# Attention on one Trainium2 core: probabilities split query-major and transposed by DMA, applied four slots later

## The chip, the cores and the metric

The kernel runs on one core of one Trainium2 chip (trn2). The metric is device time in microseconds of that core, the median of several runs; 701.6 us to 703.3 us is one and the same kernel here. A core has TensorE (PE in the rows; PEld is its weight loading), VectorE (DVE), ScalarE (ACT), GpSimd (POOL) and SyncE (SP), each with its own instruction queue, which runs strictly in the order in which it was written. They meet through semaphores. 16 DMA engines move data; in this kernel SyncE issues every transfer.

## The reference, cut to what matters

32 sequences of 256 tokens, 384 channels, 6 heads of 64. Layer norm and ReLU, masked attention, output projection, residual.

```
h = relu(layernorm(x))                        # x: 32 x 256 x 384, f32
q, k, v = heads(h @ Wq + bq), heads(h @ Wk + bk), heads(h @ Wv + bv)
scores = q @ k.T / sqrt(64)
probs = softmax(scores + where(adj, 0, -9e15))
out = x + (concat(probs @ v) @ Wf + bf)
```

## The kernel before

Every matrix product is made from f16 halves: a factor is written as hi + lo, and `three` issues the products hi·hi, hi·lo and lo·hi into one accumulator (PSUM) bank.

**A batch and its units.** The kernel goes through the 32 sequences (here: batches) one after the other. The attention of one batch is cut into six units: unit u takes the query half t = u // 3 (128 queries) and the head pair j = u % 3. For each unit `scores` makes the two 128x256 score tiles of the two heads; `mask_and_max` on VectorE adds the mask, scales, negates and keeps the row's minimum (`least`); `exps` on ScalarE makes f32 probabilities, queries on the partitions. The product with v needs keys on the partitions, so TensorE turns the four 128x128 f32 blocks of the unit with matmuls against an identity (`transpose_probs`, L834) into one of two PSUM banks; ScalarE copies that to f16 as `pt_hi` (L409, scaled by 2^14), VectorE subtracts for `pt_lo` (L543), and `apply_probs` (L850 to L852) accumulates 12 products in the bank `ctx`. A 65th column of ones in v gives the row sum; `divide` divides by it.

**The cycle and its slots.** `cycle(b)` is written out by hand for each engine. It works on batch b's attention, on the projections of batch b+1 and on the end of batch b-1, in six slots that each start with `scores(b, u)`. TensorE turns unit u-1 in slot u and applies unit u-2 in it. Between these stand the projections: `project_qk` in three pairs, `project_v` in two halves, `transpose_h` (L779, turns the normed tokens), `transpose_context` (L860) and `project_out`. Nothing but this written order and the semaphores sets what runs when. Two cycles form the body of the loop.

**The other engines.** GpSimd: `normalise`, `make_mask`, `split_lo` (the lo half of q and k, L354) and `add_bias`. ScalarE moves projections out of PSUM (`qk_full`, `v_hi_part`, `h_hi_part`, `context_hi`). VectorE makes the halves (`qk_hi_part` L559, `v_lo_part`, `h_lo_part`, `context_lo`), the layer-norm statistics (`layer_stats`) and the result (`finish`).

**SyncE.** It loads x and the mask, stores results, and places heads: `scores` contracts a head over 128 partitions, hi on one half and lo on the other, so the split projections must cross partition halves. Four transfers per head pair do this, two of 96 KB within their own partition half (L284) and two of 64 KB to the other half (L285), 12 in a batch. A transfer is issued when the queue reaches it; a wait in the queue holds all that stands behind it.

## Time and profile before

| | us |
|---|---|
| median of 3 runs | 702.35 (701.69 to 703.3) |
| span of the profiled execution | 701.6 |

| engine | busy us, share of the span |
|---|---|
| TensorE | 677.3, 97% |
| VectorE | 555.2, 79% |
| ScalarE | 464.9, 66% |
| GpSimd | 270.1, 39% |
| DMA engines | 33.8% |

Busy time of an engine is the time in which at least one of its instructions is under way. Instructions overlap by their pipelines: a duration in a row is longer than what the instruction costs in a dense sequence. That cost is the distance from its start to the start of the next, and the prediction uses it wherever a timeline shows it.

### The profile page before, as it was taken

What the parts mean: (1) busy time and instruction counts of PE and PEld (TensorE: products, weight loads), DVE (VectorE), ACT (ScalarE), POOL (GpSimd) and SP (SyncE); (2) the same over time, 40 slices, a digit from 0 to 9 for tenths busy, and PEclk for the clock granted to TensorE, in tenths of its full rate; (3) what the DMA queues carried; (4) which work ended last, traced back from release to release, by engine and by line L of the source; (5) the groups of instructions that cost most, each with busy time, mean ns of one, the idle gap of its engine ahead of it and who ended that gap; (6) DMA issues with size and microseconds to landing.
All of it is one profiled execution on the core that took longest, in us unless ns stands there. A gap on an engine that the chain in (4) does not pass through costs nothing.

```text
span 701.6 us, 21244 instructions
## 1 busy us (share of the span) xinstructions
PE 677.3 (97%) x7156; PEld 562.7 (80%) x7156; DVE 555.2 (79%) x1676; ACT 464.9 (66%) x972; POOL 270.1 (39%) x330
## 2 busy tenths in 40 slices
PE   7688999999999999999999999999999999999996
PEld 5466888888888888888888888888888888888874
DVE  5748887887887878788787878878787887888785
ACT  2545676767677676767767676776767677676763
POOL 1334444334444433444443344444334444333420
PEclk8899999999999999999999999999999999999998
DMA  5123333433332343333234333323433332343220
GB/s 187 43 52 89 101 72 89 105 85 90 90 98 71 90 105 84 90 92 96 71 91 105 84 87 94 90 74 94 105 81 89 95 88 75 95 105 78 65 71 35
DMA packets 72453, 61.36 MB, mean 87 GB/s; under 512 B 17649, under 2 KB 72434, under 8 KB 72434
## 3 DMA queue, kind: packets, MB, share of 16 engines
q1 hardware_dynamic: 72434, 61.12, 33.8%
q8 instruction: 11, 0.18, 0.1%
q14 instruction: 8, 0.07, 0.0%
HBM read 17.05 MB, written 12.58 MB: 42 GB/s over the span
## 4 chain that ended last, share of the span: by engine, by line
PE 90%; issue 3%; DVE 3%; DMA 1%; ACT 1%; POOL 1%; SPq 0%; POOLq 0%; DVEq 0%
PE ring L767 17%; PE ring L769 17%; PE ring L768 17%; PE probs_t L834 11%; PE scores L824 6%; PE scores L825 6%; PE ctx L850 3%; PE ctx L852 3%; PE ctx L851 3%; PE ring L779 3%; PE ring L860 3%; DMA w_raw<-in_L_gnn_Wv_dram 1%; ACT probs L404 0%; DMA x_in<-in_x_dram 0%; DVE w_lo L623 0%
## 5 line engine op out<-in xcount | busy, mean ns | idle before, releaser
L404 ACT ACTIVATE probs<-logits,least 128x256 f32<-128x256 f32 x384 | 175.1, 504 | 78.0 <-DVE least L536 77.0
L354 POOL TENSOR_TENSOR split<-qk,split 128x512 f16<-128x512 f32 x96 | 111.3, 1160 | 274.9 <-DVE split L559 274.9
L409 ACT ACTIVATE pt_hi<-probs_t 128x512 f16<-128x512 f32 x192 | 114.6, 597 | 108.1 <-PE probs_t L834 107.3
L536 DVE CUSTOM_DVE_ANT_0 logits<-scores,mask,logit_unscale 128x256 f32<-128x256 f32 x384 | 169.1, 478 | 4.5 <-PE scores L825 3.7
L767 PE MATMUL ring<-h_hi,w_hi 128*128 128x256 f16 x576 | 158.3, 275 | 2.0 <-DVE w_lo L623 1.5
L768 PE MATMUL ring<-h_lo,w_hi 128*128 128x256 f16 x576 | 158.1, 275 | 0.0
L769 PE MATMUL ring<-h_hi,w_lo 128*128 128x256 f16 x576 | 158.0, 274 | 0.0
L543 DVE SCALAR_TENSOR_TENSOR pt_lo<-probs_t,pt_hi 128x512 f16<-128x512 f32 x192 | 131.6, 686 | 0.7 <-ACT pt_hi L409 0.6
L834 PE MATMUL probs_t<-ident,probs 128*128 128x128 f32 x768 | 116.4, 274 | 5.4 <-ACT probs L404 5.3
L559 DVE CAST split<-qk 128x512 f16<-128x512 f32 x96 | 41.3, 430 | 98.3 <-ACT qk L422 98.3
L422 ACT ACTIVATE qk<-ring,qk_bias_s,qkv_ratio 128x256 f32<-128x256 f32 x192 | 96.7, 552 | 15.2 <-PE ring L769 15.2
L824 PE MATMUL scores<-heads 128*128 128x256 f16 x384 | 94.9, 274 | 4.6 <-DMA heads<-split 3.9
L834 PEld LDWEIGHTS probs_t<-ident,probs 128*128 128x128 f32 x768 | 89.9, 141 | 9.4 <-issue 6.5
L362 POOL TENSOR_TENSOR residual<-x_in,bf_full 128x384 f32<-128x384 f32 x64 | 62.7, 1001 | 90.2 <-DVE result L588 83.4
L825 PE MATMUL scores<-heads 128*128 128x256 f16 x384 | 94.5, 273 | 0.0
L851 PE MATMUL ctx<-v_lo,pt_hi 128*128 128x64 f16 x768 | 89.4, 192 | 0.0
L852 PE MATMUL ctx<-v_hi,pt_lo 128*128 128x65 f16 x768 | 89.3, 193 | 0.0
L850 PE MATMUL ctx<-v_hi,pt_hi 128*128 128x65 f16 x768 | 89.2, 194 | 0.0
L850 PEld LDWEIGHTS ctx<-v_hi,pt_hi 128*128 128x128 f16 x768 | 72.1, 97 | 4.4
L851 PEld LDWEIGHTS ctx<-v_lo,pt_hi 128*128 128x128 f16 x768 | 70.9, 98 | 5.5
L852 PEld LDWEIGHTS ctx<-v_hi,pt_lo 128*128 128x128 f16 x768 | 71.0, 97 | 0.0
L767 PE MATMUL ring<-w_hi,ct_hi 128*128 128x384 f16 x192 | 62.8, 327 | 2.2 <-DVE ct_lo L579 2.2
(86 smaller groups left out, 1300.0 us busy)
## 6 DMA issues: line engine op xcount, KB each, us to landing
heads<-split SPq DMA_DIRECT2D x192, 96.0 KB, 2.2
x_in<-in_x_dram SPq DMA_DIRECT2D x32, 384.0 KB, 3.3
heads<-split SPq DMA_DIRECT2D x192, 64.0 KB, 2.1
out_dram<-result SPq DMA_DIRECT2D x64, 192.0 KB, 1.9
adj_in<-in_adj_dram SPq DMA_DIRECT2D x32, 64.0 KB, 2.0
w_raw<-in_L_gnn_Wq_dram SPq DMA_DIRECT2D x1, 576.0 KB, 4.1
w_raw<-in_L_gnn_Wk_dram SPq DMA_DIRECT2D x1, 576.0 KB, 6.5
w_raw<-in_L_gnn_Wv_dram SPq DMA_DIRECT2D x1, 576.0 KB, 6.3
```

Of the source, the lines that this page charges most:

```text
L404: act.activation(probs[u % 2][:, a], logits[u % 2][:, a], ACT.Exp, bias=least[u % 2][:, a:a + 1], scale=-1.0).then_inc(probs_ready, 1)
L536: dve.tensor_tensor_reduce(out=logits[u % 2][:, a], in0=score_bank[u % 2][:, a * S:(a + 1) * S], in1=mask[b.parity][:, t], scale=logit_uns ...
L543: dve.scalar_tensor_tensor(out=pt_lo[u % 2][:].rearrange("p a t q -> p (a t q)"), in0=pt_bank[u % 2][:], scalar=P_SCALE, in1=pt_hi[u % 2][ ...
L767: pe.matmul(out_ap, a_hi, m_hi, start=first, stop=False)
L768: pe.matmul(out_ap, a_hi, m_lo, start=False, stop=False)
L769: return pe.matmul(out_ap, a_lo, m_hi, start=False, stop=last)
L824: pe.matmul(o, q, h[:, 1], start=True, stop=False)
L825: mm = pe.matmul(o, q, h[:, 2], start=False, stop=True)
L834: mm = pe.transpose(pt_bank[u % 2][:, o:o + P], probs[u % 2][:, a, s * P:(s + 1) * P], ident[:])
L850: pe.matmul(ctx_ps[:, h], hi, vh, start=(s == 0), stop=False)
L851: pe.matmul(ctx_ps[:, h, 0:D], hi, vl, start=False, stop=False)
L852: mm = pe.matmul(ctx_ps[:, h], lo, vh, start=False, stop=(s == QT - 1))
```

## The change

The probabilities are no longer turned by TensorE. `exps` takes its bias from `raised` = `least` + ln(2^14), which a new small VectorE instruction makes, so the probabilities come out scaled. Then, still query-major in SBUF, ScalarE copies them to f16 (`p_rows[u][:, 0]`) and GpSimd makes the lo half (`probs_lo`, `p_rows[u][:, 1]`). SyncE issues one DMA transpose per unit, 128 partitions by 1024 f16 values (256 KB), which lands in `p_cols[u]`; `apply_probs` reads that. Each unit has buffers of its own. `apply_probs` of unit u stands in slot u+4 (`LAG`), not u+2.

The two PSUM banks of the turned probabilities join the ring (three banks become five), and many PSUM tiles have another bank. x and the residual have four buffers, the normed halves two. The 64 KB crossing transfers of heads are gone; `copy_heads` makes two VectorE copies in their place for each head pair, from one partition half to the other. All six queues' orders are rewritten, one more cycle runs at the end, and the loop body holds four cycles.

```diff
+        logits = [sb(f"logits{u}", [P, 2, S], F32) for u in range(3)]
+        least = [sb(f"least{u}", [P, 2], F32) for u in range(3)]
+        raised = [sb(f"raised{u}", [P, 2], F32) for u in range(3)]
+        probs = [sb(f"probs{u}", [P, 2, S], F32) for u in range(3)]
+        p_rows = [sb(f"p_rows{u}", [P, 2, 2, S], F16) for u in range(UNITS)]
+        p_cols = [sb(f"p_cols{u}", [P, 2, 2, QT, P], F16) for u in range(UNITS)]
...
-        ring = [bank("ring0"), bank("ring1"), bank("ring2")]
...
+        R_QK = [ring[0], ring[3], ring[2]]
+        R_V = [ring[3], ring[2]]
+        R_CT = [ring[1], ring[4]]
+        R_OUT = [ring[1], ring[4]]
...
-            for k in (-1, 0):
+            for k in range(-1, FIRST_IN_LOOP):
                 cycle(Batch(0, k))
...
-                cycle(Batch(i, 1))
-                cycle(Batch(i, 2))
-            for k in range(2 * TURNS + 1, B + 1):
+                for n in range(RING):
+                    cycle(Batch(i, FIRST_IN_LOOP + n))
+            for k in range(FIRST_IN_LOOP + RING * TURNS, B + 2):
                 cycle(Batch(0, k))
...
             def store(b, t):
                 wait(sp, result_ready, b.count(2, t + 1))
+                alone(sp)
                 sp.dma_start(out_v[b.index(), t], result[t][:]).then_inc(out_stored[t], 16)
             def place_heads(b, j):
                 wait(sp, qk_hi_ready, b.count(C, j + 1))
                 wait(sp, qk_lo_ready, b.count(C, j + 1))
+                alone(sp)
                 for a in range(2):
                     own = slice(D * a, D * a + D)
-                    other = slice(D - D * a, 2 * D - D * a)
                     dst, src = heads[b.parity][:, 2 * j + a], split[j]
                     sp.dma_start(dst[own], src[own, 1:4]).then_inc(heads_placed[j], 16)
-                    sp.dma_start(dst[other, 0:2], src[own, 0:3:2]).then_inc(heads_placed[j], 16)
+            def transpose_probs(b, u):
+                wait(sp, p_lo_ready, b.count(UNITS, u + 1))
+                alone(sp)
+                sp.dma_start_transpose(p_cols[u][:].rearrange("p w a s q -> p (w a s) q"),
+                                       p_rows[u][:].rearrange("p w a k -> p (w a k)")).then_inc(p_placed[u], 16)
...
             def cycle(b):
-                if (b + -1).exists():
-                    store(b + -1, 0)
-                if (b + 3).exists() and (b + 1).exists():
+                here, before, front = b.exists(), (b + -1).exists(), (b + 1).exists()
+                if before:
+                    transpose_probs(b + -1, 4)
+                if b.exists():
+                    place_heads(b, 2)
+                if before:
+                    transpose_probs(b + -1, 5)
+                if here:
+                    transpose_probs(b, 0)
+                if here and (b + 4).exists():
+                    wait(sp, residual_ready, b.count(2, 2))
+                    alone(sp)
+                    load_x(b + 4)
+                if (b + -2).exists():
+                    store(b + -2, 1)
+                if here:
+                    transpose_probs(b, 1)
+                if (b + 3).exists() and front:
                     wait(sp, mask_ready, (b + 1).count(2, 2))
+                    alone(sp)
                     load_adj(b + 3)
                 if (b + 1).exists():
-                    place_heads(b + 1, 0)
-                    place_heads(b + 1, 1)
-                if (b + -1).exists():
-                    store(b + -1, 1)
+                    place_heads((b + 1), 0)
+                if here:
+                    transpose_probs(b, 2)
                 if (b + 1).exists():
-                    place_heads(b + 1, 2)
-                if (b + 3).exists() and (b + 1).exists():
-                    wait(sp, residual_ready, (b + 1).count(2, 2))
-                    load_x(b + 3)
+                    place_heads((b + 1), 1)
+                if here:
+                    transpose_probs(b, 3)
+                if before:
+                    store(b + -1, 0)
...
+            def probs_lo(b, u):
+                wait(pool, p_hi_ready, b.count(UNITS, u + 1))
+                pool.tensor_tensor(p_rows[u][:, 1], probs[u % 3][:], p_rows[u][:, 0],
+                                   ALU.subtract).then_inc(p_lo_ready, 1)
...
+                if here:
+                    split_lo(b, 2)
+                if before:
+                    probs_lo(b + -1, 5)
+                if here:
+                    probs_lo(b, 0)
+                if (b + 2).exists():
+                    normalise(b + 2)
+                if here:
+                    probs_lo(b, 1)
                 if front:
                     make_mask(b + 1)
                     split_lo(b + 1, 0)
...
+                if here:
+                    probs_lo(b, 2)
+                if front:
                     split_lo(b + 1, 1)
-                    if not first:
-                        add_bias(b + 1)
-                if (b + 2).exists():
-                    normalise(b + 2)
-                if front:
...
+                if here:
+                    probs_lo(b, 3)
+                if front:
+                    add_bias(b + 1)
+                if here:
+                    probs_lo(b, 4)
...
             def exps(b, u):
+                wait(act, p_lo_ready, b.count(UNITS, u - 2))
+                wait(act, raised_ready, b.count(UNITS, u + 1))
                 for a in range(2):
-                    wait(act, logits_ready, b.count(2 * UNITS, 2 * u + a + 1))
-                    act.activation(probs[u % 2][:, a], logits[u % 2][:, a], ACT.Exp,
-                                   bias=least[u % 2][:, a:a + 1], scale=-1.0).then_inc(probs_ready, 1)
+                    act.activation(probs[u % 3][:, a], logits[u % 3][:, a], ACT.Exp,
+                                   bias=raised[u % 3][:, a:a + 1], scale=-1.0).then_inc(probs_ready, 1)
             def probs_hi(b, u):
-                wait(act, pt_ready, b.count(UNITS, u + 1))
-                act.activation(pt_hi[u % 2][:].rearrange("p a t q -> p (a t q)"), pt_bank[u % 2][:],
-                               ACT.Copy, scale=P_SCALE).then_inc(pt_hi_ready, 1)
+                wait(act, probs_ready, b.count(2 * UNITS, 2 * u + 2))
+                act.activation(p_rows[u][:, 0], probs[u % 3][:], ACT.Copy).then_inc(p_hi_ready, 1)
...
+                wait(dve, probs_ready, b.count(2 * UNITS, 2 * u - 4))
...
-            def probs_lo(b, u):
-                wait(dve, pt_hi_ready, b.count(UNITS, u + 1))
-                dve.scalar_tensor_tensor(
-                    out=pt_lo[u % 2][:].rearrange("p a t q -> p (a t q)"), in0=pt_bank[u % 2][:],
-                    scalar=P_SCALE, in1=pt_hi[u % 2][:].rearrange("p a t q -> p (a t q)"),
-                    op0=ALU.mult, op1=ALU.subtract).then_inc(pt_lo_ready, 1)
+                        op0=ALU.add, op1=ALU.min, accum_out=least[u % 3][:, a:a + 1]).then_inc(logits_ready, 1)
+                dve.wait_ge(logits_ready, b.count(2 * UNITS, 2 * u + 2))
+                dve.tensor_scalar(raised[u % 3][:], least[u % 3][:], P_RAISE, None, ALU.add).then_inc(raised_ready, 1)
...
+            def copy_heads(b, j):
+                wait(dve, qk_lo_ready, b.count(C, j + 1))
+                for a in range(2):
+                    own = slice(D * a, D * a + D)
+                    other = slice(D - D * a, 2 * D - D * a)
+                    dst, src = heads[b.parity][:, 2 * j + a], split[j]
+                    dve.tensor_copy(dst[other, 0:2], src[own, 0:3:2]).then_inc(heads_copied, 1)
...
                 if here:
                     mask_and_max(b, 0)
+                if before:
+                    divide(b + -1, 0)
                 if front and not first:
                     h_lo_part(b + 1)
-                lo_of(0)
-                if before:
-                    finish(b + -1, 0)
...
                 if here:
                     mask_and_max(b, 1)
-                lo_of(1)
-                if front:
-                    qk_hi_part(b + 1, 0)
+                    copy_heads(b, 2)
+                    v_lo_part(b, 0)
+                    v_lo_part(b, 1)
...
-            def transpose_probs(b, u):
-                wait(pe, pt_lo_ready, b.count(UNITS, u - 1))
-                for a in range(2):
-                    wait(pe, probs_ready, b.count(2 * UNITS, 2 * u + a + 1))
-                    for s in range(QT):
-                        o = (a * QT + s) * P
-                        mm = pe.transpose(pt_bank[u % 2][:, o:o + P], probs[u % 2][:, a, s * P:(s + 1) * P],
-                                          ident[:])
-                mm.then_inc(pt_ready, 1)
             def apply_probs(b, u):
                 t, j = u // C, u % C
-                wait(pe, pt_lo_ready, b.count(UNITS, u + 1))
...
-                        hi, lo = pt_hi[u % 2][:, a, s], pt_lo[u % 2][:, a, s]
+                        hi, lo = p_cols[u][:, 0, a, s], p_cols[u][:, 1, a, s]
                         vh, vl = v_hi[b.parity][:, s, h], v_lo[b.parity][:, s, h]
                         pe.matmul(ctx_ps[:, h], hi, vh, start=(s == 0), stop=False)
...
+                def attend(u):
+                    if here:
+                        scores(b, u)
+                    if u < LAG:
                         if before:
-                            transpose_probs(b + -1, UNITS - 1)
+                            apply_probs(b + -1, UNITS - LAG + u)
                     elif here:
-                        transpose_probs(b, u - 1)
...
+                        apply_probs(b, u - LAG)
+                attend(0)
                 if front and not first:
                     transpose_h(b + 1)
+                if here:
+                    project_v(b, 1)
+                attend(1)
+                if front:
+                    project_qk(b + 1, 0)
+                attend(2)
+                if before:
+                    transpose_context(b + -1, 0)
+                if front:
+                    project_qk(b + 1, 1)
+                attend(3)
+                if b.k == 1:
+                    pe.wait_ge(w_lo_ready, 10)
                 if before:
                     project_out(b + -1, 0)
-                if here:
...
-                if front:
...
+                    project_qk(b + 1, 2, (0,))
...
+                attend(4)
+                if before:
+                    transpose_context(b + -1, 1)
+                if front:
+                    project_qk(b + 1, 2, (1,))
+                    project_v(b + 1, 0, (0,))
+                attend(5)
+                if front:
+                    project_v(b + 1, 0, (1, 2))
                 if before:
                     project_out(b + -1, 1)
-                apply_of(3)
```

The order of the instructions shows this at three places. First TensorE, the start of a slot behind the loop, before (`probs_t` is the PSUM bank of turned probabilities, `ident` the identity):

```order
L824 MATMUL scores<-heads 128x256
L825 MATMUL scores<-heads 128x256
L824 MATMUL scores<-heads 128x256
L825 MATMUL scores<-heads 128x256
L834 MATMUL probs_t<-ident,probs 128x128 x4
L767 MATMUL ring<-h_hi,w_hi 128x256
L768 MATMUL ring<-h_lo,w_hi 128x256
```

and after, the same place:

```order
L874 MATMUL scores<-heads 128x256
L875 MATMUL scores<-heads 128x256
L874 MATMUL scores<-heads 128x256
L875 MATMUL scores<-heads 128x256
L890 MATMUL ctx<-v_hi,p_cols 128x65
L891 MATMUL ctx<-v_lo,p_cols 128x64
L892 MATMUL ctx<-v_hi,p_cols 128x65
```

The row of four transposes (L834) is gone between the scores and what follows.

GpSimd, one batch behind the loop, before (`split` is the lo half of q and k, `residual` is x plus bias):

```order
L348 TENSOR_SCALAR mask<-adj_in,mask_scale 128x256 x2
L354 TENSOR_TENSOR split<-qk_0,split 128x2x256
L354 TENSOR_TENSOR split<-qk_1,split 128x2x256
L362 TENSOR_TENSOR residual<-x_in,bf_full 128x384 x2
L334 TENSOR_TENSOR rstd<-var_s,half 128x2
L339 TENSOR_SCALAR normed<-x_in,neg_mean,rstd 128x384 x2
L354 TENSOR_TENSOR split<-qk_2,split 128x2x256
```

and after:

```order
L391 TENSOR_TENSOR split<-qk_2,split 128x2x256
L405 TENSOR_TENSOR p_rows<-probs,p_rows 128x512 x2
L371 TENSOR_TENSOR rstd<-var_s,half 128x2
L376 TENSOR_SCALAR normed<-x_in,neg_mean,rstd 128x384 x2
L405 TENSOR_TENSOR p_rows<-probs,p_rows 128x512
L385 TENSOR_SCALAR mask<-adj_in,mask_scale 128x256 x2
L391 TENSOR_TENSOR split<-qk_0,split 128x2x256
L405 TENSOR_TENSOR p_rows<-probs,p_rows 128x512
L391 TENSOR_TENSOR split<-qk_1,split 128x2x256
L405 TENSOR_TENSOR p_rows<-probs,p_rows 128x512
L400 TENSOR_TENSOR residual<-x_in,bf_full 128x384 x2
L405 TENSOR_TENSOR p_rows<-probs,p_rows 128x512
```

Six instructions on `p_rows` have come in between, and the batch starts with `split` of its own third head pair, which before stood last.

SyncE, the queue of one batch behind the loop, before:

```order
L274 DMA out_dram<-result 128x384
L284 DMA heads<-split 64x768
L285 DMA heads<-split 64x2x256
L284 DMA heads<-split 64x768
L285 DMA heads<-split 64x2x256
L284 DMA heads<-split 64x768
L285 DMA heads<-split 64x2x256
L284 DMA heads<-split 64x768
L285 DMA heads<-split 64x2x256
L274 DMA out_dram<-result 128x384
L284 DMA heads<-split 64x768
L285 DMA heads<-split 64x2x256
```

and after:

```order
L298 DMA_TRANSPOSE p_cols<-p_rows 128x8x128
L292 DMA heads<-split 64x768 x2
L298 DMA_TRANSPOSE p_cols<-p_rows 128x8x128 x2
L274 DMA x_in<-in_x_dram 128x2x384
L282 DMA out_dram<-result 128x384
L298 DMA_TRANSPOSE p_cols<-p_rows 128x8x128
L277 DMA adj_in<-in_adj_dram 128x2x256
L292 DMA heads<-split 64x768 x2
L298 DMA_TRANSPOSE p_cols<-p_rows 128x8x128
L292 DMA heads<-split 64x768 x2
L298 DMA_TRANSPOSE p_cols<-p_rows 128x8x128
L282 DMA out_dram<-result 128x384
```

Twelve head transfers have become six, and six transposes stand among them in one queue.

## Rows read from the trace of the kernel before

**Rows 1.** The page: busy time of each engine, and its share in 40 slices.

```profile
PE 677.3 (97%) x7156; PEld 562.7 (80%) x7156; DVE 555.2 (79%) x1676; ACT 464.9 (66%) x972; POOL 270.1 (39%) x330
...
PEclk8899999999999999999999999999999999999998
```

**Rows 2.** Busy time by stretch: PE, PEld, DVE, ACT, POOL, clock, DMA share, GB/s.

```profile
100.00:600.00 500.00, 500.00 (x5414) 420.68 (x5412) 408.83 (x1245) 349.12 (x733) 203.37 (x245) 1.00 0.35 90
```

**Rows 3.** The chain that ended last, 300 to 343 us: start, length, piece.

```profile
by line: PE ring L767 19.0%; PE ring L769 19.0%; PE ring L768 19.0%; PE probs_t L834 13.2%; PE scores L824 6.6%; PE scores L825 6.6%; PE ctx L850 3.5%; PE ctx L852 3.5%; PE ctx L851 3.5%; PE ring L779 3.2%; PE ring L860 3.0%
...
306.19 0.33 PE ring L860 x3
...
307.32 0.44 PE probs_t L834 x4
308.12 0.69 PE ring L779 x6
...
327.82 0.44 PE probs_t L834 x4
```

**Rows 4.** TensorE in order of time: start us, duration us, instruction.

```profile
303.33 0.19 PE L850 MATMUL ctx<-v_hi,pt_hi 128*128 128x65 f16 x1
...
303.69 0.28 PE L824 MATMUL scores<-heads 128*128 128x256 f16 x1
...
304.13 0.60 PE L834 MATMUL probs_t<-ident,probs 128*128 128x128 f32 x4
304.56 0.33 PE L767 MATMUL ring<-w_hi,h_hi 128*128 128x384 f16 x1
```

**Rows 5.** VectorE in order of time, the same columns.

```profile
304.80 0.18 DVE L571 RECIPROCAL inv_sum<-ctx 128x6 f32<-128x6 f32 x1
305.02 0.56 DVE L573 TENSOR_TENSOR context<-ctx,inv_sum 128x384 f32<-128x384 f32 x1
305.49 0.47 DVE L536 CUSTOM_DVE_ANT_0 logits<-scores,mask,logit_unscale 128x256 f32<-128x256 f32 x1
...
306.30 0.68 DVE L543 SCALAR_TENSOR_TENSOR pt_lo<-probs_t,pt_hi 128x512 f16<-128x512 f32 x1
...
310.29 0.68 DVE L543 SCALAR_TENSOR_TENSOR pt_lo<-probs_t,pt_hi 128x512 f16<-128x512 f32 x1
310.89 0.61 DVE L588 SCALAR_TENSOR_TENSOR result<-ring,out_unscale,residual 128x384 f32<-128x384 f32 x1
...
314.19 0.43 DVE L559 CAST split<-qk 128x512 f16<-128x512 f32 x1 [1.28 <-ACT qk L422]
314.54 0.19 DVE L571 RECIPROCAL inv_sum<-ctx 128x6 f32<-128x6 f32 x1
```

**Rows 6.** Groups by line: busy us, mean ns of one, idle before and its releaser.

```profile
L404 ACT ACTIVATE probs<-logits,least 128x256 f32<-128x256 f32 x384 | 175.1, 504 | 78.0 <-DVE least L536 77.0
...
L409 ACT ACTIVATE pt_hi<-probs_t 128x512 f16<-128x512 f32 x192 | 114.6, 597 | 108.1 <-PE probs_t L834 107.3
L354 POOL TENSOR_TENSOR split<-qk,split 128x512 f16<-128x512 f32 x96 | 111.3, 1160 | 274.9 <-DVE split L559 274.9
```

**Rows 7.** SyncE's queue in order of time: start, time to issue, transfer.

```profile
307.02 0.47 SPq L284 DMA_DIRECT2D heads<-split  x1
307.54 0.62 SPq L285 DMA_DIRECT2D heads<-split  x1
...
309.66 0.45 SPq L267 DMA_DIRECT2D x_in<-in_x_dram  x1
311.69 0.36 SPq L274 DMA_DIRECT2D out_dram<-result  x1
```

**Rows 8.** The page: transfers, count, KB each, median us from issue to landing.

```profile
heads<-split SPq DMA_DIRECT2D x192, 96.0 KB, 2.2
x_in<-in_x_dram SPq DMA_DIRECT2D x32, 384.0 KB, 3.3
heads<-split SPq DMA_DIRECT2D x192, 64.0 KB, 2.1
```

274 lines of the change are left out of this document (107 added, 167 removed).

## The prediction, made before the changed kernel ran

> **What bounds the kernel now.** I read the busy times first: TensorE is busy 677.3 us of 701.6 [rows 1], and from 100 to 600 us it is busy 500.00 us of 500, at the full granted clock, 2.4 GHz [rows 2]. A busy TensorE could still be one that waits inside its pipeline, so I read the chain of waits next: from 300 to 343 us it is made of TensorE pieces alone, and 13.2% of it is L834, the transposes of the probabilities [rows 3]. The order of time says what they cost: four of them start at 304.13, and the next instruction starts at 304.56 [rows 4]; the chain gives the same four 0.44 us [rows 3]. Last the period: the same four transposes stand at 307.32 and, one batch later, at 327.82 [rows 3], so a batch takes 20.50 us. 32 batches are 656.0 us; 45.6 us of the span lie outside of that, in start and end. Every other engine has room: over the 500 us VectorE is busy 408.83 (16.8 us a batch), ScalarE 349.12 (14.3), GpSimd 203.37 (8.3), the DMA engines 35% at 90 GB/s [rows 2].
>
> **TensorE's share of the change.** Removed are 6 x 0.44 = 2.64 us a batch. Nothing is added there, and the products keep their number and size. The period would be 17.86 us if TensorE stayed without a gap. The order after gives slots of nearly equal length: with 0.44 us for scores and 0.36 for applying (303.33 to 303.69), 0.163 for a product 384 wide, 0.109 for one 256 wide (from scores, 0.44 / 4), 0.69 for turning h and 0.33 for a context [rows 3, 4], they come to 2.97, 2.77, 3.10, 3.26, 2.61 and 3.26 us, a sum of 17.97.
>
> **VectorE.** `probs_lo` goes: 310.29 to 310.89 is 0.60 us, six times 3.6 us. `raised` comes, six times. It waits for VectorE's own result, as the product after the reciprocal does: that pair costs 0.22 us from 304.80 to 305.02 [rows 5], and I take this 0.22 for wait and instruction, 1.3 us a batch. Six copies of 512 f16 values on 64 partitions come; nearest is the cast of 512 values, 0.35 us from 314.19 to 314.54 [rows 5]. I take it as the upper end, 2.1 us in all; the lower is half of that. VectorE then needs 16.8 - 3.6 + 1.3 + 2.1 = 16.6 us of 17.86, or 93% (15.5 at the lower end). This is the tightest engine that a row can price.
>
> **GpSimd and ScalarE.** GpSimd gets `probs_lo`, a subtraction of the very form of L354, 1160 ns [rows 6]: 6 x 1.16 = 7.0, in all 15.3 us of 17.86, 86%. What hides it is the idle time before L354, 274.9 us in this run [rows 6]; but only 2.6 us a batch would be left. ScalarE exchanges one 128x512 copy for another, out of SBUF in place of PSUM; L409 takes 597 ns [rows 6], and I take no difference: 14.3 us of 17.86.
>
> **SyncE and the DMA engines.** No row shows a DMA transpose. Plain issues cost SyncE 0.36 us (a store) to 0.62 us (a crossing transfer of heads) [rows 7]. Six remaining head transfers at about 0.55, two stores at 0.36, x at 0.45 and the mask at about a store's price come to 4.8 us a batch. Six transposes of x us each add 6x. The queue keeps up with 17.86 us while x is below (17.86 - 4.8) / 6 = 2.2 us, and with the old period below 2.6. From the rows, one transpose costs 0.36 us if it is one plain push; it costs 8 x 0.36 = 2.9 us if the sequencer pushes each of its eight 128x128 blocks like a store (at 0.62, 5.0 us). I take a value under 2.2, nearer to a plain instruction, because one instruction is issued; this is the weakest choice here. In bytes: 90 GB/s at 35% means some 257 GB/s if the engines were full. A batch moves 1.85 MB now; less 6 x 64 KB [rows 8], plus 6 x 256 KB, it is 3.0 MB, or 11.8 us of engine time at that rate, 66% of 17.86. If bytes of a transpose cost n times those of a copy, the engines fill up at n = 2.0, and reach the old period at n = 2.4.
>
> The Trainium skill speaks to the issue price: DMA: Bandwidth & Descriptors, the section on fast HWDGE, gives 262,144 cycles for 8,192 tiles when each tile is pushed, so 32 cycles a tile. With its tile of 16 partitions by 128 values a unit has 64 tiles, 2,048 cycles, at SyncE's 1.2 GHz (Trainium Kernel Development and Optimization, NeuronCore Architecture) an estimate of 1.7 us; the queue would need 4.8 + 10.2 = 15.0 us, and the forecast would stand. No row here shows it.
>
> **The latency that four slots must cover.** Take unit 2, the tightest that I laid out. Its scores end 6.2 us into the cycle; mask and minimum cost 0.81 us (305.49 to 306.30), `raised` 0.22 [rows 5]; ScalarE makes its exponentials (two at 504 ns [rows 6]) behind q and k of pair 0, until about 8.8. Its hi half stands behind q and k of pair 1, until about 10.5; GpSimd is held by the mask and `split` until about 11.3, and has the lo half at 12.4. TensorE applies it in slot 0 of the next cycle, at 17.86 + 0.44 = 18.3. So 5.9 us are left for issue, queue and landing. Plain transfers of 96 and 384 KB land in 2.2 and 3.3 us [rows 8]; 256 KB lies between, about 2.8, plus up to 2.2 of issue: 5.0, which fits. The other units come out at 5.5 to 6.5. Behind unit 4's transpose in the queue stand the heads of pair 2; the same layout has them landed about 1 us before their scores. If a transpose takes over 5.9 us, TensorE stalls, and the period stretches by 6/4 of the excess.
>
> **Start and end.** In the last batch nothing covers the chain from the last scores: the transpose by DMA (2.8 us) and GpSimd's 1.16 us stand in place of TensorE's 0.44 us and VectorE's 0.60, with the issue about +4 us. The start does not change in size. Sum: 701.6 - 84.5 (192 x 0.44) + 4 = 621.1 us of span. The median of the runs lies 0.7 above the profiled span, so 621.8; I say 622. In general, time = 50.3 + 32 x period.
>
> **The rivals.**
> - *TensorE stays the bound*, as above. For it: four engines and the queue add up to less than 17.86 us each by rows or bounds. Against it: VectorE at 93% and GpSimd at 86% in strict order. 612 to 640 us: 612 if the period is 17.7 and the end costs nothing, 640 if it is 18.4. Chance 0.50.
> - *An engine in between becomes the bound.* VectorE waits in its queue for q and k from ScalarE (1.28 us before the cast at 314.19 [rows 5]); with 1.3 us of spare time a batch, two such waits that remain stretch the batch to about 19.0 us: 50.3 + 608 = 658 us. Or a transpose takes 7 us in place of 5: +1.1 x 6/4 = 1.7 us, a period of 19.5, 674 us. 640 to 699 us, chance 0.20.
> - *The transposes are the bound, and the kernel is slower than before.* The place is SyncE's queue, or the DMA engines behind it. It decides from x = 2.6 us or n = 2.4. At the rows' eight pushes, x = 2.9, the period is 4.8 + 17.4 = 22.2 us: 761 us. For it: the engine was never seen doing this, heads and transposes share one queue, and a late transpose holds the heads too. Chance 0.22; about half of it lies at or under 765 us.
> - *A price per 128x128 block.* If each block costs the engines more than 1 us and the blocks of a unit do not overlap, a unit takes over 8 us, a batch over 48, the kernel over 1586 us. Chance 0.05. The Trainium skill has such a figure: DVE Perf Modes, The three transpose paths, lists 1309 ns for one block by DMA beside 390 ns for TensorE, and its rules prefer TensorE where PSUM will do. By 1309 ns, unoverlapped, a batch would take an estimated 63 us. This kernel's TensorE needs 109 ns a block (0.44 / 4), and that time goes away altogether.
> - *Two effects cancel*, within 0.2% of before (which is about what a measurement of this kernel can tell from no change): 0.03.
>
> **How the numbers follow.** 622 us is the time of the likeliest case, whose own range is 612 to 640. Faster is its 0.50 with the 0.20 of the second: 0.70. Same 0.03. Slower is 0.22 + 0.05 = 0.27. The range goes from 612 to 765: left out are some 0.02 below, and 0.16 above (half of the third rival and the fourth).
>
> **What would show it.** Right: in the steady stretch TensorE is busy nearly without a gap, scores of the same unit repeat after 17.9 us, no L834 in the chain, and transposes land within 5.9 us. VectorE would stand near 93% and GpSimd near 86%. Wrong: TensorE's waits name a DMA on `p_cols` (latency or bytes), `heads` (the queue), or VectorE's `raised`, `context` or `h_lo`; SyncE's queue shows transposes above 2.2 us each without idle time; the granted clock falls because TensorE pauses. If VectorE's copies cost over 0.55 us each, VectorE alone passes 17.86 us.

## The result, and the profile after

The changed kernel takes 754.89 us (median of 4 runs, 752.65 to 756.02) against 702.83 us beside it: 1.073 times the time before, 95% interval 1.071 to 1.075. The forecast was 622 us and faster. In the prediction's own formula the period is (754.9 - 50.3) / 32 = 22.0 us a batch, in place of 20.5 before and 17.86 forecast.

The page after, busy times, clock, and the chain that ended last, by engine and by line (compare [rows 1]):

```profile
PE 636.1 (84%) x6388; PEld 488.9 (65%) x6388; DVE 659.5 (88%) x1868; ACT 464.1 (62%) x972; POOL 501.4 (67%) x522
...
PEclk8868999999999999999999999999999999999998
...
DVE 54%; issue 28%; PE 10%; DMA 2%; ACT 2%; DVEq 2%; POOL 1%; SPq 1%; POOLq 0%; ACTq 0%
```

The stretch from 100 to 600 us, columns as in [rows 2], and from the groups by line of the same stretch GpSimd's lo halves, whose count gives the batches:

```profile
100.00:600.00 500.00, 435.05 (x4502) 335.28 (x4500) 455.06 (x1298) 324.63 (x684) 354.65 (x363) 0.97 0.65 138
```

```profile
L405 POOL TENSOR_TENSOR p_rows<-probs,p_rows 128x512 f16<-128x512 f32 x136 | 159.5, 1173 | 81.7 <-ACT p_rows L471 79.7
```

136 / 6 = 22.7 batches, so 22.06 us each. A batch costs VectorE 455.06 / 22.7 = 20.1 us (forecast 16.6), ScalarE 14.3 (14.3), GpSimd 15.6 (15.3). TensorE, which was never idle in [rows 2], is idle for 65 us of the 500, and the transposes L834 of [rows 3] are gone. Who waited for whom in the same stretch (us in total, times, longest):

```profile
ACT probs L466 <- DVE raised L595: 158.8, 116, 3.3
PE ring L817 <- DVE ct_lo L637: 37.8, 23, 2.5
```

ScalarE waits for VectorE's `raised`, TensorE for VectorE's `ct_lo` (the lo half of the context). TensorE's granted clock is 0.97 in the stretch (1.00 before); a chain that is VectorE's hangs little on it. What made VectorE dear is in the page's groups (busy us, mean ns of one) and in the statistics of the two lines (durations in ns, min/median/max):

```profile
L617 DVE COPY heads<-split 64x512 f16<-64x512 f16 x192 | 114.1, 594 | 18.3 <-POOL split L391 12.4
L595 DVE TENSOR_SCALAR raised<-least 128x2 f32<-128x2 f32 x192 | 98.7, 514 | 6.6
```

```profile
L617 DVE COPY heads<-split x192: 285/291/1236, 28.4 to 725.6; 64x512 f16<-64x512 f16 x192
```

```profile
L595 DVE TENSOR_SCALAR raised<-least x192: 168/264/1143, 34.4 to 736.2; 128x2 f32<-128x2 f32 x192
```

A copy can take 0.29 us and a `raised` 0.17, and both reach over 1.1 us. In order of time (start, duration) one sees when:

```profile
305.96 0.17 DVE L595 TENSOR_SCALAR raised<-least 128x2 f32<-128x2 f32 x1
...
307.81 1.16 POOL L405 TENSOR_TENSOR p_rows<-probs,p_rows 128x512 f16<-128x512 f32 x1
...
308.73 0.26 DVE L595 TENSOR_SCALAR raised<-least 128x2 f32<-128x2 f32 x1
...
312.20 0.61 DVE L617 COPY heads<-split 64x512 f16<-64x512 f16 x2
...
318.24 1.15 POOL L405 TENSOR_TENSOR p_rows<-probs,p_rows 128x512 f16<-128x512 f32 x1 [0.18 <-ACT p_rows L471]
318.31 0.08 DVE L590 DVE_READ_ACCUMULATOR2_ANT least<- 128x1 f32 x1
318.42 1.00 DVE L595 TENSOR_SCALAR raised<-least 128x2 f32<-128x2 f32 x1
...
319.45 0.91 ACT L466 ACTIVATE probs<-logits,raised 128x256 f32<-128x256 f32 x2 [1.29 <-DVE raised L595]
...
320.47 1.45 DVE L617 COPY heads<-split 64x512 f16<-64x512 f16 x2
320.52 1.26 POOL L391 TENSOR_TENSOR split<-qk,split 128x512 f16<-128x512 f32 x1 [1.12 <-DVE split L608]
```

GpSimd's L405 ends at 307.81 + 1.16 = 308.97, and the `raised` begun at 308.73 ends at 308.99. The next L405 ends at 319.39, the `raised` of 318.42 at 319.42: two values a partition, 1.00 us. With GpSimd idle the same instruction took 0.17. ScalarE's exponentials wait behind it.

The whole trace says the same. Of the 192 `raised`, 106 took over 0.25 us, and each of these ended 0.02 to 0.03 us after the end of a GpSimd instruction; the 47 during which GpSimd was idle took at most 0.17. Of the 192 copies, 95 took over 0.30 us, and each ended 0.15 us after the end of a GpSimd instruction. All 95 had begun inside L391, L400 or L405 of GpSimd, and no copy that began inside one of these was spared. The 59 copies that began inside GpSimd's L371 (a power of 128x2 values, some 0.74 us) took 0.29 all the same. Not every instruction of VectorE is held either: of the 384 minima (L590), which read PSUM, 244 began beside a running GpSimd instruction, and none took over 0.49 us (mean 477 ns, 478 before). Of the 64 L655, the batch-norm statistics, which read SBUF, 28 did, and none took over 0.56 (mean 549 ns, 548 before).

The transposes are innocent at first sight: median landing from the page, and two issues from SyncE's queue:

```profile
p_cols<-p_rows SPq DMA_TRANSPOSE x192, 3.1
```

```profile
303.53 1.24 SPq L298 DMA_TRANSPOSE p_cols<-p_rows  x1
305.12 0.38 SPq L282 DMA_DIRECT2D out_dram<-result  x1
305.69 1.25 SPq L298 DMA_TRANSPOSE p_cols<-p_rows  x1
```

### The profile page after: what moved, and what is told of

Same layout as the page of the kernel before. It is cut to its first block, busy times and chain, and to the rows that moved or that the text cites. A ratio compares the mean times of both kernels' runs of the same rounds, so it can differ in the third digit from the quotient of the medians.

```text
span 753.1 us, 20054 instructions
## 1 busy us (share of the span) xinstructions
PE 636.1 (84%) x6388; PEld 488.9 (65%) x6388; DVE 659.5 (88%) x1868; ACT 464.1 (62%) x972; POOL 501.4 (67%) x522
## 4 chain that ended last, share of the span: by engine, by line
DVE 54%; issue 28%; PE 10%; DMA 2%; ACT 2%; DVEq 2%; POOL 1%; SPq 1%; POOLq 0%; ACTq 0%
DVE logits L590 17%; DVE heads L617 10%; DVE raised L595 6%; DVE split L608 3%; DVE ct_lo L637 3%; DVE stats L655 3%; DVE v_lo L621 3%; PE ring L817 2%; DVE h_lo L600 2%; PE ring L819 2%; PE ring L818 2%; ACT probs L466 2%; DVE least L590 1%; DVE result L646 1%; DVE w_lo L684 1%
## 5 line engine op out<-in xcount | busy, mean ns | idle before, releaser
L466 ACT ACTIVATE probs<-logits,raised 128x256 f32<-128x256 f32 x384 | 174.2, 500 | 223.9 <-DVE raised L595 222.7
L405 POOL TENSOR_TENSOR p_rows<-probs,p_rows 128x512 f16<-128x512 f32 x192 | 225.2, 1173 | 121.8 <-ACT p_rows L471 119.7
L590 DVE CUSTOM_DVE_ANT_0 logits<-scores,mask,logit_unscale 128x256 f32<-128x256 f32 x384 | 169.1, 477 | 36.2 <-PE scores L875 34.7
L391 POOL TENSOR_TENSOR split<-qk,split 128x512 f16<-128x512 f32 x96 | 114.1, 1189 | 74.8 <-DVE split L608 74.8
L617 DVE COPY heads<-split 64x512 f16<-64x512 f16 x192 | 114.1, 594 | 18.3 <-POOL split L391 12.4
L471 ACT ACTIVATE p_rows<-probs 128x512 f16<-128x512 f32 x192 | 120.0, 625 | 3.1
L890 PE MATMUL ctx<-v_hi,p_cols 128*128 128x65 f16 x768 | 91.6, 197 | 27.5 <-DVE context L631 25.0
L817 PE MATMUL ring<-w_hi,ct_hi 128*128 128x384 f16 x192 | 65.0, 338 | 50.3 <-DVE ct_lo L637 50.3
L595 DVE TENSOR_SCALAR raised<-least 128x2 f32<-128x2 f32 x192 | 98.7, 514 | 6.6
L890 PEld LDWEIGHTS ctx<-v_hi,p_cols 128*128 128x128 f16 x768 | 73.0, 99 | 39.8 <-DVE context L631 17.2
L891 PE MATMUL ctx<-v_lo,p_cols 128*128 128x64 f16 x768 | 91.5, 194 | 0.0
L892 PE MATMUL ctx<-v_hi,p_cols 128*128 128x65 f16 x768 | 91.4, 195 | 0.0
L891 PEld LDWEIGHTS ctx<-v_lo,p_cols 128*128 128x128 f16 x768 | 72.2, 100 | 2.1
L892 PEld LDWEIGHTS ctx<-v_hi,p_cols 128*128 128x128 f16 x768 | 72.2, 99 | 0.0
L817 PEld LDWEIGHTS ring<-h_hi,w_hi 128*128 128x128 f16 x576 | 58.3, 101 | 18.9 <-DVE h_lo L600 7.3
L400 POOL TENSOR_TENSOR residual<-x_in,bf_full 128x384 f32<-128x384 f32 x64 | 64.2, 1023 | 6.9 <-issue 6.9
```

The lines of the kernel that those rows point to most:

```text
L405: pool.tensor_tensor(p_rows[u][:, 1], probs[u % 3][:], p_rows[u][:, 0], ALU.subtract).then_inc(p_lo_ready, 1)
L466: act.activation(probs[u % 3][:, a], logits[u % 3][:, a], ACT.Exp, bias=raised[u % 3][:, a:a + 1], scale=-1.0).then_inc(probs_ready, 1)
L471: act.activation(p_rows[u][:, 0], probs[u % 3][:], ACT.Copy).then_inc(p_hi_ready, 1)
L590: dve.tensor_tensor_reduce(out=logits[u % 3][:, a], in0=score_bank[u % 2][:, a * S:(a + 1) * S], in1=mask[b.parity][:, t], scale=logit_uns ...
L595: dve.tensor_scalar(raised[u % 3][:], least[u % 3][:], P_RAISE, None, ALU.add).then_inc(raised_ready, 1)
L617: dve.tensor_copy(dst[other, 0:2], src[own, 0:3:2]).then_inc(heads_copied, 1)
```

## The experiments

The theory: **GpSimd, now busy 71% of the steady stretch (354.65 of 500), holds VectorE's copies, casts and `raised`, all from SBUF to SBUF, until its own instruction ends, and VectorE's queue is the path**. Rivals: the transposes (queue, bytes, latency); VectorE's plain amount of work; the written order. The kernel before, timed beside the runs, lay at 702.2 to 703.2 us; the edits are shown shortened.

### Is it the hold?

**`raised` as two 128x1 instructions** in place of one 128x2. The same result and one instruction more; statistics as above.

```diff
-dve.tensor_scalar(raised[u % 3][:], least[u % 3][:], P_RAISE, None, ALU.add)
+for a in range(2):
+    dve.tensor_scalar(raised[u % 3][:, a:a + 1], least[u % 3][:, a:a + 1], P_RAISE, None, ALU.add)
```

> Edit: the 128x2 instruction for raised becomes two of 128x1, on the same engine. Theory (GpSimd holds VectorE's one-source SBUF instructions, and an instruction with a single value per partition is not held): the mean of L595 falls from 514 ns to about 170, VectorE loses some 1.5 us a batch, 700 to 725 us. Rival A (VectorE is overloaded by the added instructions themselves): one more instruction per unit, 0.1 us each, 765 to 775 us. If single-value instructions are held as well: each unit still waits once, 755 to 775 us, and the mean of the pair is uneven. Rival B (DMA transposes and their latency bound the kernel): unchanged, 755 us.

```profile
L596 DVE TENSOR_SCALAR raised<-least x384: 142/149/156, 36.2 to 696.1; 128x1 f32<-128x1 f32 x192
```

712.1 us (ratio 1.012, 1.009 to 1.014): 43 us of the loss of 52 are gone by splitting one small instruction. No instance is held any more. The hold moved in part: the cast rose from 466 to 651 ns in the mean, the copies from 594 to 614.

**GpSimd's lo half on 16 of 256 columns.**

```diff
-pool.tensor_tensor(p_rows[u][:, 1], probs[u % 3][:], p_rows[u][:, 0], ALU.subtract)
+pool.tensor_tensor(p_rows[u][:, 1, :, 0:16], probs[u % 3][:, :, 0:16], p_rows[u][:, 0, :, 0:16], ALU.subtract)
```

> Edit: GpSimd's probs_lo works on 16 of 256 columns of each head (the lo halves of the other columns are left zero, so part of the product is left out). VectorE's instructions are all unchanged. Theory: with GpSimd rarely busy, raised falls from 514 to about 200 ns and the copies from 594 to about 330 ns, VectorE gets some 4 us a batch back: 630 to 665 us. Rival A (VectorE overloaded by its own work): durations stay at 514 and 594, the time stays above 735 us. Rival C (GpSimd's latency in the unit's chain): the time falls, but the durations of VectorE's instructions stay.

```profile
L599 DVE TENSOR_SCALAR raised<-least 128x2 f32<-128x2 f32 x192 | 33.1, 172 | 6.7
```

664.3 us (0.943, 0.938 to 0.949), at the edge of the theory's band, and `raised` is back at 172 ns with VectorE's code unchanged. The copies fall only to 442 ns, not to 330: GpSimd is still busy 53% of the stretch. So 91 us hang on how long GpSimd works. That could also be GpSimd's shorter latency in the chain of a unit (rival C), but VectorE's busy time falls by 93 us (659.5 to 566.1) and its idle time does not fall (94 us before the edit, 98 after it), so what was saved is VectorE's held time.

**The kernel before with a busy GpSimd:** six idle subtractions of 128x512 a batch.

```diff
+pool.tensor_tensor(spare_lo[:], spare_in[:], spare[:], ALU.subtract)      # six a batch
```

> Edit: the kernel before, with six more GpSimd subtractions of 128x512 a batch into a spare tile that nobody reads. It asks whether GpSimd's load alone costs, where VectorE has few instructions that GpSimd can hold (three casts and two small ones a batch) and 18% idle time. Theory: L559 (the cast, 427 ns) rises to 500 ns or more, the other VectorE durations stay, the time stays within 1%: 702 to 710. Rival E (any GpSimd load slows VectorE's instructions or the memory as a whole): the PSUM-reading ones (L536, 478 ns) get longer too and the time goes above 720.

717.5 us (1.020, 1.019 to 1.022), between the two expectations, and the cast did not rise. From 100 to 600 us none of VectorE's groups changes: the cast takes 427 ns in both kernels, the layer norm's small 128x2 instruction 169 in both, the minimum 478 and 477. Of the 96 casts 64 find GpSimd idle and 29 meet its power instruction of 128x2 values, beside which they keep their 427 ns. So VectorE hardly meets GpSimd's long instructions in this order, and the run does not test the hold. It shows what GpSimd's load alone costs: 20.61 us a batch against 20.50 (from the first minimum of batch 4 to that of batch 28), some 3.5 us in all. 12 of the 15 us lie in the first four batches (102.4 us against 90.4). The changed kernel loses 1.5 us in each batch.

**Two inputs in place of one.** `raised` adds a tile with ln(2^14):

```diff
-dve.tensor_scalar(raised[u % 3][:], least[u % 3][:], P_RAISE, None, ALU.add)
+dve.tensor_tensor(raised[u % 3][:], least[u % 3][:], lift[:], ALU.add)
```

> The changed kernel, raised made by adding a second tile that holds ln(2^14) (two inputs) in place of adding a constant (one input). Theory (the hold by GpSimd strikes instructions with one input of more than one value a partition): raised falls from 514 ns to 170 to 200 ns, and the kernel to 700 to 715 us, about the 712.1 us of the two 128x1 instructions. Rival (the hold goes with the wait for its own result or with the size of the tile, not with the form): raised stays over 400 ns and the kernel near 755 us.

735.2 us (1.046, 1.043 to 1.049), outside of both expectations, and the instruction stays held, at 507 ns in the mean. Why 20 us are gone all the same stays open: VectorE's busy time fell by 8 us (copies 568 ns, cast 440), the rest is idle time of it. The next kernel also gives the copies and casts two inputs (`ALU.max` of a value and itself).

> As the last, and VectorE's copies of heads and its casts of q and k have two inputs as well (the larger of a value and itself). Theory: none is held any more; each costs a flat 0.5 to 0.6 us, as h_lo with its 512 values does (0.55), against 0.61 and 0.65 us in the mean with raised in two parts: 685 to 705 us. Rival (what the one-input forms gain when GpSimd is idle, 0.29 us a copy, outweighs what the hold costs): 712 us or more.

```profile
L596 DVE TENSOR_TENSOR raised<-least,lift x192: 160/247/1099, 34.9 to 717.9; 128x2 f32<-128x2 f32 x192
```

```profile
L618 DVE TENSOR_TENSOR heads<-split x192: 418/452/1360, 30.6 to 754.7; 64x512 f16<-64x512 f16 x192
```

The first row is of the kernel before this one, the second of the last: 782.4 us (1.114, 1.111 to 1.117), on the rival's side. A free copy costs 0.42 to 0.45 us in this form, and it is held as well. My theory of the form was wrong; the hold is not one for one-input instructions. What escapes it here are the instructions that read PSUM, the batch-norm statistics, and one value a partition. The Trainium skill, SBUF — State Buffer, Who interferes with whom, speaks of both forms: copies, casts and tensor_scalar in their two-port modes shut out GpSimd and are shut out by it for a whole instruction, and a two-input instruction with both inputs in SBUF contends with GpSimd's reads. The rows agree on VectorE's side: 1.00 us against 0.17 with one input, up to 1.10 against 0.16 with two. GpSimd loses little where it comes second: L391 takes 1.26 us where a copy had begun 0.05 us before it, 1.16 without one. By that rule a copy beside GpSimd's L371 would be held too; the 59 above were not, and here the measurement decides.

### Is it the transposes?

**No transposes at all:** the products read `p_rows` as it lies (another product, the same number of matmuls), and wait for the lo half.

```diff
-sp.dma_start_transpose(p_cols[u]..., p_rows[u]...).then_inc(p_placed[u], 16)
-hi, lo = p_cols[u][:, 0, a, s], p_cols[u][:, 1, a, s]
+hi, lo = p_rows[u][:, 0, a, s * P:(s + 1) * P], p_rows[u][:, 1, a, s * P:(s + 1) * P]
```

> Edit: the DMA transposes are left out; the products read the query-major halves directly (so the product is another one; the same instructions on TensorE). Theory: transposes are hidden, 745 to 757 us. Rival B (the transposes' issue, bytes or latency bound the kernel): it falls to 640 to 700 us.

751.8 us (1.070, 1.066 to 1.073) with `raised` at 507 and copies at 599 ns. The transposes cost at most some 3 us of 755: the single times of the two kernels overlap (749.6 to 753.8 and 752.7 to 756.0).

### Can the copies go elsewhere?

**Back to SyncE's crossing transfers:**

```diff
+sp.dma_start(dst[other, 0:2], src[own, 0:3:2]).then_inc(heads_placed[j], 16)
-dve.tensor_copy(dst[other, 0:2], src[own, 0:3:2]).then_inc(heads_copied, 1)
```

> Edit: the VectorE copies of crossing head halves are undone, SyncE issues the six 64 KB transfers again; the transposes stay. Theory: VectorE loses 114 us of copies (594 ns each, of which 290 are work), the other waits stay: 660 to 700 us. Rival A (overload by work alone): 6 x 0.29 us a batch go, 56 us: about 700 us. Rival B (queue and DMA engines bound the kernel): twelve head transfers beside six transposes make the queue longer by 6 x 0.6 us: 770 us or more.

750.7 us (1.062, 1.054 to 1.071; single times from 742 to 757): my 660 to 700 was far off. VectorE falls from 88% to 74%, `raised` stays at 506 ns, but the chain is now SyncE's:

```profile
SPq 47%; issue 15%; DVE 13%; PE 11%; DMA 10%; POOL 2%; ACT 1%; DVEq 1%; POOLq 0%; ACTq 0%
```

**To ScalarE, with `raised` in two parts:**

```diff
+act.activation(dst[other, 0:2], src[own, 0:3:2], ACT.Copy).then_inc(heads_copied, 1)
-dve.tensor_copy(dst[other, 0:2], src[own, 0:3:2]).then_inc(heads_copied, 1)
```

> Edit: both, raised as two instructions of 128x1, and the copies on ScalarE. Theory: VectorE needs (18.9 us a batch with raised in two) - 3.7 = 15.2 us, ScalarE 17.0 to 17.5, GpSimd 15.6, TensorE 17.86: 630 to 670 us, faster than the kernel before the change. Rival D (SyncE's queue or the latency of the unit's chain takes over): 680 to 710.

733.6 us (1.044, 1.042 to 1.046), 21 us worse than with the copies on VectorE and above both expectations. A copy costs ScalarE 628 ns, and the chain divides among three engines: ScalarE 26%, VectorE 25%, TensorE 21%. The same move with `raised` unchanged:

> Edit: the copies of crossing head halves go from VectorE to ScalarE; SyncE's queue stays as in the changed kernel, raised stays one 128x2 instruction. Theory (VectorE is the bound, and what it waits for GpSimd is part of its time): VectorE loses the 114 us of copies, ScalarE (464 us busy) gets 6 x 0.4 to 0.5 us a batch and has room: 670 to 710 us; L595 still near 500 ns. Rival A (VectorE's own work alone): 755 - 56 = about 700. Rival D (after VectorE the next bound is hit at once, as SyncE's queue was with the crossing transfers): 735 to 750.

770.8 us (1.097, 1.095 to 1.099), a miss: all three expectations lay at 750 or below, and it is worse than the changed kernel itself. And with `raised` in two and GpSimd's lo half cut to 16 columns:

> Edit: as the run with both, and GpSimd's probs_lo on 16 of 256 columns of each head (the other lo halves are zero, part of the product left out). It asks whether TensorE's own 17.86 us a batch, the 622 us of the prediction, is reached once neither VectorE nor GpSimd holds anything up. If so: 618 to 632 us. If the transposes or ScalarE (17 us of 17.86) bound it: 640 to 660.

727.1 us (1.034, 1.033 to 1.036), a miss again (618 to 632, or 640 to 660) and hardly better than 733.6. With `raised` never held and GpSimd busy 47% of the stretch, the hold cannot be what is left; ScalarE, 81% busy, has the largest share of the chain (30%, VectorE 27%). That the order binds here is argued, not shown. Wherever the copies went, the engine or queue that took them took a large share of the chain.

### What does one part cost in the kernel before?

**The copies alone** (the transfers L285 gone, six VectorE copies a batch, behind `context_lo`, `finish` and `context_lo`):

> The kernel before, with one part of the change alone: the six 64 KB crossing transfers of heads a batch are VectorE copies. GpSimd is busy 39% of the time here, so a copy should cost 0.3 to 0.45 us in the mean (free ones took 0.29, held ones up to 1.24). VectorE then needs 16.8 + 6 x 0.4 = 19.2 us of 20.5. Theory (GpSimd's holding needs a busy GpSimd): 703 to 710 us, same or a little slower. Rival (the copies alone bring the loss, by their place in VectorE's order ahead of the minimum): over 715 us, with TensorE waiting for VectorE.

796.4 us (1.135, 1.133 to 1.137), on the side of the rival (over 715), though nobody had expected 94 us. The statistics of the copies, and the chain:

```profile
L567 DVE COPY heads<-split x192: 285/290/1234, 27.6 to 770.5; 64x512 f16<-64x512 f16 x192
```

```profile
DVE 40%; issue 33%; ACT 19%; PE 2%; DVEq 1%; POOL 1%; DMA 1%; ACTq 1%; SPq 0%; POOLq 0%
```

94.2 / 32 = 2.94 us a batch, and six copies at their mean of 495 ns are 2.97: **all of it comes through**, though VectorE had 3.7 us of idle time a batch before. In this run it is idle 3.5 us a batch still (500 - 424.60 = 75.4 us over 21.3 batches). Most of that is waits for ScalarE, which an addition elsewhere does not use:

```profile
DVE split L558 <- ACT qk L421: 56.4, 64, 0.9
```

**The same copies, directly ahead of such waits:**

```diff
+                    copy_heads(b + 1, 0)
                     qk_hi_part(b + 1, 1)
...
+                    copy_heads(b + 1, 1)
                     qk_hi_part(b + 1, 2)
...
+                    copy_heads(b + 1, 2)
                     v_lo_part(b + 1, 1)
```

> The kernel before with the six VectorE copies in place of the crossing transfers, as in the run that took 796.4 us, but each pair of copies stands directly ahead of an instruction for which VectorE waits on ScalarE (the casts of pairs 1 and 2, waited for 0.9 us each, and the second v_lo). Theory (the 94 us came from the place: copies ahead of the next minimum delay the exponentials, and the waits for ScalarE stay beside them): the copies fill the waits, and at least half of the 94 us goes: 715 to 750 us, with less idle time before the casts. Rival (VectorE and ScalarE pass work to and fro with no slack, wherever VectorE's extra work stands): 780 us or more.

733.8 us (1.044, 1.042 to 1.046), as the theory had it: two thirds of the 94 us went with their place. 12 us of these are the copies themselves, which meet less of GpSimd's work there (432 ns in the mean, 495 before the move).

**`raised` alone** (an addition of 0, for which the exponentials wait):

> The kernel before with raised alone added, as an addition of 0 (so that the result stays the same), and the exponentials wait for it. GpSimd is busy 39%, so an instruction should cost some 0.17 us and the wait for its own result about 0.1. Theory (the kernel before has a second chain, VectorE with its waits for ScalarE, that is as long as TensorE's): 6 x 0.2 to 0.3 us a batch come through whole, 740 to 760 us. Rival (VectorE's 3.7 us of idle time a batch take it up, TensorE stays the bound): 702 to 710 us.

778.2 us (1.107, 1.105 to 1.110), 2.35 us a batch, more than expected. It is hardly held here (168/168/999 ns, mean 191), so the hold is not the reason. The kernel before, then this one, in order of time:

```profile
305.49 0.47 DVE L536 CUSTOM_DVE_ANT_0 logits<-scores,mask,logit_unscale 128x256 f32<-128x256 f32 x1
305.89 0.08 DVE L536 DVE_READ_ACCUMULATOR2_ANT least<- 128x1 f32 x1
...
306.01 0.51 ACT L404 ACTIVATE probs<-logits,least 128x256 f32<-128x256 f32 x1 [0.65 <-DVE least L536]
```

```profile
306.59 0.47 DVE L538 CUSTOM_DVE_ANT_0 logits<-scores,mask,logit_unscale 128x256 f32<-128x256 f32 x1
...
307.40 0.08 DVE L538 DVE_READ_ACCUMULATOR2_ANT least<- 128x1 f32 x1
307.51 0.27 DVE L543 TENSOR_SCALAR raised<-least 128x2 f32<-128x2 f32 x1
...
307.81 0.91 ACT L406 ACTIVATE probs<-logits,raised 128x256 f32<-128x256 f32 x2 [1.15 <-DVE raised L543]
```

Before, the first exponential started 0.52 us after the first minimum began, beside the second minimum; with `raised` 1.22 us after it. To tell that delay from VectorE's own 0.3 us, **the exponentials wait for both halves, and nothing is added**:

```diff
+wait(act, logits_ready, b.count(2 * UNITS, 2 * u + 2))
 for a in range(2):
-    wait(act, logits_ready, b.count(2 * UNITS, 2 * u + a + 1))
```

> The kernel before, no instruction added: the exponential of a unit's first half waits for the minimum of both halves. That starts ScalarE's pair of exponentials some 0.41 us later a unit; with raised it is 0.70 us later (1.22 in place of 0.52 us after the first minimum starts). Theory (the loop VectorE, exponentials, q and k, cast has no slack, so ScalarE's delay counts): 0.41 / 0.70 of the 75 us that raised cost, 730 to 750 us. Rival (it is VectorE's own 0.31 us a unit that counts, 60 of the 75 us): 702 to 712 us.

```profile
307.35 0.47 DVE L536 CUSTOM_DVE_ANT_0 logits<-scores,mask,logit_unscale 128x256 f32<-128x256 f32 x1
...
308.27 0.91 ACT L404 ACTIVATE probs<-logits,least 128x256 f32<-128x256 f32 x2 [1.19 <-DVE least L536]
```

738.0 us (1.051, 1.049 to 1.053), inside the theory's band. The first exponential starts 0.92 us after the first minimum, some 0.41 us later than before, and this costs 36 us with no work added; of 6 x 0.41 = 2.5 us a batch 1.1 come through. So the kernel before had a second path nearly as long as TensorE's. By the lines of the chain with `raised` alone (minimum 20%, q and k on ScalarE 11%, exponentials 9%, cast 3%) it runs minimum, exponentials, q and k on ScalarE, cast on VectorE, next minimum.

### The changed kernel without `raised`

The exponentials take `least` as their bias, each half when its own is ready; the scaling by 2^14 is left out.

```diff
-wait(act, raised_ready, b.count(UNITS, u + 1))
+    wait(act, logits_ready, b.count(2 * UNITS, 2 * u + a + 1))
-bias=raised[u % 3][:, a:a + 1]
+bias=least[u % 3][:, a:a + 1]
```

> Left out of the work: the scaling of the probabilities by 2^14 (the bias of the exponential is the row's minimum itself, and raised is not made). Each half's exponential waits for its own logits. Theory (VectorE's one-source instructions are held while GpSimd works, and the chain through raised bounds the kernel): all 98.7 us of raised go, and what remains held are the copies and the casts. With two unheld 128x1 instructions in its place the kernel took 712.1 us, with 41.2 us of VectorE for them; without them I expect 680 to 700 us, VectorE's busy time near 580. Rival (the step that GpSimd's holding costs is only moved, from raised to casts and copies): 705 to 715 us, no better than with the two instructions, with copies above 620 ns and the cast above 650.

698.7 us (0.995, 0.993 to 0.997). So `raised` costs 56 of the 755: 43 go when it is made as two instructions that are not held, 13 more when it is gone with its wait. The time is the theory's, the durations are the rival's: the copies (687 ns) and the cast (721) are held more than in the changed kernel. Next, **pair 2 crosses by DMA again**, pairs 0 and 1 stay copies:

> As the kernel without raised (the scaling by 2^14 is left out), and the crossing transfer of head pair 2 goes back to two DMAs from SyncE; pairs 0 and 1 stay VectorE copies. Theory: 2 of 6 copies leave VectorE (some 1.2 us a batch of held time, half of it on the path), and SyncE's queue gets 2 x 0.6 us, which it can bear since pairs 0 and 1 add nothing: 665 to 690 us, at least 10 us under the kernel without raised. Rival (a queue delay as with all six crossings on SyncE, 750.7 us): 700 us or more, with TensorE's scores waiting for the heads' DMA.

694.4 us (0.990, 0.985 to 0.994). This and the last are the two that compute the attention of all columns in less time than the kernel before, by 1% and 0.5%, the scaling apart, whose worth no run here measures. Against the last it gains 4 us, where at least 10 were expected. With **GpSimd's lo half on 16 columns** on top:

> As the last, and GpSimd's lo half of the probabilities covers 16 of 256 columns of each head (that part of the product is left out, and so is the scaling by 2^14). Asks how near the kernel comes to TensorE's own limit (17.86 us a batch, 622 us) when neither raised, nor the long GpSimd subtraction, nor all six copies stand in the way. Theory: 625 to 645 us, TensorE busy over 490 us of the 500 from 100 to 600 us. Rival (strict order and latency of the exponentials bound it in any case): 650 us or more, with the same waits for probs that the changed kernel has.

661.9 us (0.943, 0.941 to 0.945), not the 625 to 645 that I expected. TensorE holds 59% of the chain and SyncE's queue 12%. GpSimd's long lo halves cost 32 us here, and even without them 622 us is not reached. Last, an attempt at tuning, **`context_lo` ahead of the copies of pair 1**, since TensorE waited for it:

```diff
+                    context_lo(b + -1, 1)
                     copy_heads(b + 1, 1)
-                    context_lo(b + -1, 1)
```

> The changed kernel without raised (the scaling by 2^14 is left out) and with head pair 2 crossing by DMA (694.4 us), with one swap in VectorE's order: the second context_lo of a batch goes ahead of the held copies of pair 1. TensorE waited 25.0 us of 500 for ct_lo, 1.0 us a batch. Theory (that wait is on the path): 665 to 685 us. Rival (the copies, now later, delay the minimum of the next unit as before, and TensorE waits for heads or context in its place): 690 to 698 us.

709.8 us (1.011, 1.009 to 1.012), 15 us more than without the swap and above both expectations. The copies' mean rose from 755 ns to 914:

```profile
L617 DVE COPY heads<-split 64x512 f16<-64x512 f16 x128 | 117.0, 914 | 7.7 <-POOL split L393 3.7
```

One place further back they are held longer. That this rise makes up the 15 us was not tested by itself (128 x 0.16 = 20 us of VectorE's time).

## Why the prediction was wrong, point by point

- **TensorE's share** was right in kind (L834 is gone), and useless: the period was set elsewhere. TensorE was idle 13% of the stretch.
- **VectorE: the step that failed.** The forecast priced a copy at 0.35 us at most and `raised` with its wait at 0.22, from rows of a kernel whose GpSimd was busy 41% of the stretch. They measured 0.59 and 0.51: 6 x 0.24 + 6 x 0.29 = 3.2 of the 3.5 us by which 20.1 passes 16.6. The prediction gave 0.55 us a copy as the point at which VectorE passes 17.86 us, and it did; but it had no mechanism for it. The change puts 7 us of work on GpSimd and SBUF-to-SBUF work on VectorE at once, and the price of the one depends on the other. The split into two instructions (-43 us) and the short lo half (-91 us) show it.
- **"Four engines and the queue add up to less than 17.86 us each"** was the second failure. VectorE's 79% busy was read as 21% to spare. The spare time was the waits of a loop through two engines, and there was hardly any slack in it: the copies alone cost 94 us, their full duration, `raised` alone 75, a mere wait 36. With 93% forecast, there was no room for the 3.5 us of waits. The exponential that no longer starts on its own half was not priced at all; the term for `raised` had only VectorE's side.
- **GpSimd, ScalarE:** 15.6 and 14.3 us measured, 15.3 and 14.3 forecast. Right in size; the harm was in what a busy GpSimd does to its neighbour.
- **SyncE and the DMA engines:** x was 1.24 us, under the 2.2 that the forecast wanted and under the estimate of 1.7 us from the figure of the Trainium skill (DMA: Bandwidth & Descriptors, the section on fast HWDGE); 3.1 us to land, in all at most 4.3 of the 5.9 us budget. The bytes came out as 138 GB/s x 22.06 = 3.04 MB a batch (3.0 forecast). The eight pushes (2.9 us) and the price per block (over 8 us a unit) are refuted, and without transposes the time is nearly the same.
- **The rivals.** The measured 755 lies beside the third rival's 761 by chance: that rival's cause, the transposes, is worth at most some 3 us. The second named the right kind (an engine in between) but not the way. It had VectorE wait for q and k from ScalarE; that wait bound the kernel before with the parts added to it, while in the changed kernel VectorE's cast (L608) waits 0.0 us and ScalarE waits for VectorE. It gave this 640 to 699 us, since it took the waits as two of about 0.6 us in a batch with spare time. The range held the time; its reason did not.
- **What would show it wrong** served well: ScalarE's waits name VectorE's `raised`, TensorE's name its `context` and `ct_lo`, and none in the stretch names `p_cols`.

Not settled: how the 52 us divide among hold, copies and order in the changed kernel itself, since each part taken away changes what the others meet, and the new order as a whole was never run without the new instructions; why two inputs for `raised` gave 20 us; and what holds the last kernel but one at 662 us.

## What to carry to other kernels

Idle time of an engine is spare only if it can be used where the new work must stand: look at what ends each of its waits, and whether that engine waits for the first one in turn. A small instruction between a producer and a waiting engine costs its latency and the overlap that it breaks, here 0.70 us a time for 0.17 us of work. Before moving work to GpSimd, list what VectorE does from SBUF to SBUF and where the two would meet; in these runs instructions that read PSUM, the batch-norm statistics and single values a partition escaped.
